# A six-block decoder layer on one NeuronCore: biases padded to 128 rows or moved off TensorE, gathered rows loaded up front, router and context products mixed

## The chip, the cores and the metric

The kernel runs on one core of one Trainium2 chip. The metric is the device time of one execution in microseconds (us), less is better. A core has five engines with instruction streams of their own: TensorE (PE; its weight loads are shown apart as PEld), VectorE (DVE), ScalarE (ACT), GpSimd (POOL) and SyncE (SP, shown as SPq where it issues DMAs). They run side by side and wait for one another by semaphores. All data is fp32, and TensorE runs one fp32 product as two passes, so the profile counts two matmul instructions for one line of code.

## The reference

Input x is (4, 1024, 256), ctx (4, 77, 256); with 128 partitions (P), 4096 tokens are 32 tiles (NT) or 8 chunks (NCH) of 4 tiles (TC). D is 256, in KD = 2 blocks of 128.

```python
x = x + mamba(_layernorm(x))
x = x + gelu_product(_layernorm(x), ctx)     # h = x ctx^T; (gelu(h) * h) ctx
x = x + top1_experts(_layernorm(x))          # 8 experts
x = x + self_attention(_layernorm(x))        # 16 heads, causal
x = x + cross_attention(_layernorm(x), ctx)  # q, k, v, o with biases
x = x + top2_experts(_layernorm(x))          # 8 experts, SwiGLU, 1024 wide

def _L0_ffn_ref(x, router_w, router_b, expert_w, expert_b):
    logits = hs @ router_w + router_b
    probs = softmax(logits);  idx = argmax(probs);  gate = probs[idx]
    return gate * (hs @ expert_w[idx] + expert_b[idx])
```

The second router has a bias of the same kind (`logits = xf @ wg.T + bg`), and cross attention ends in `out @ Wo.T + bo`.

## The kernel before, in words

The residual (`K.resid`, R in the code) stays in SBUF through all stages, [128, 32, 256]. The stages run one after another, each in a block of its own that ends in a barrier of all engines. In a block each engine has its stream written out by hand, and the order in it is fixed.

`_context_and_route` (L913) computes the second residual block and the first router in one loop over chunks. For chunk n TensorE's stream is: `hidden(n)` (xnT by ctxT into pH), the transposes of chunk n+1's normalised rows and of chunk n-1's second normalised rows, `product(n)` (L1260: four tiles of gT by the rows of ctx into pO, which must be added to R before the next one), `logits(n-1)` (L1268: for each of four tiles a bias product with one row, `ones[0:1]` by `router_b`, and two router products into 8 columns), and `places(n-2)` (L1278: prefix counts of the tokens of each expert, with `base`, the first slot of each expert, added by a product with one row). VectorE adds pO to R (L1028), takes statistics of the new rows, finds the largest logit (L1032, L1036), and computes the choice (L1042 to L1056), then the shift (L1018) from which ScalarE normalises (L1182), evaluates Gelu (L1189) and copies the transposed rows (L1174: xnT, hT). VectorE makes gT from it (L1024). The transposes, logits and places share four PSUM banks `pT` in turn (`USES`, `BANKS`); the banks are copied out by ScalarE. Rows go to DRAM sorted by expert by indirect DMAs of GpSimd.

`_expert_units` (L1315) runs the expert product over 39 units of 128 sorted rows, each with one expert's weights. SyncE reads a unit's row and expert number from a table into registers and issues the loads of h (L1347) and w (L1349) into four buffers; ScalarE copies the transposed rows; TensorE does the transposes of the next unit (L1399), then the bias product (L1406) of 8 rows, `mine[:, i]` (1 in the row of the unit's expert) by `b` [8, 256], and the two weight products (L1410). VectorE scales by the gate, GpSimd scatters to `y1_tokens`.

`_project_qkv` (L1435) has chunk loops on all engines: y, the expert output of 4 tiles, is loaded from `y1_tokens` by SyncE (`front`, L1454), added to R by VectorE (`gather`, L1475), normalised and transposed (`LayerNormFront`), projected by q, k and v (L1499, L1502), and v is stored to DRAM by SyncE (`tail`, L1463: four DMAs a chunk). SyncE's order is front(i+1), tail(i). VectorE's order puts the gather and the statistics of chunk i+1 ahead of the evictions of chunk i's first tile.

`_cross_attention` (L2171) is pipelined by tile over 32 tiles. TensorE: transposes and queries, scores, the product with v (L2700), `product` (output bias with one row, L2708, and two products by wo, L2710), the second router (`logits`, L2733 and L2735) and its places. VectorE adds to R (L2323). GpSimd normalises (`normalise`), spreads, and scatters. The sorted rows feed `_expert_slots` (L2811), and `_combine` (L2971) ends the kernel.

## Time and profile before

| | |
|---|---|
| time, median of 3 runs | 3711.72 us (3709.19 to 3711.99) |
| profiled execution | 3711.74 us, span 3709.9 us |
| TensorE busy | 3152.7 us, 85% of the span |
| VectorE busy | 2068.2 us, 56% |
| ScalarE busy | 1450.1 us, 39% |
| GpSimd busy | 1447.2 us, 39% |
| mean granted clock of TensorE | 0.894 of 2.4 GHz |
| DMA | 351.36 MB, mean 95 GB/s |

Stages by the trace: Mamba to about 1037 us, `_context_and_route` to 1213, `_expert_units` to 1366, `_project_qkv` to 1581, self-attention to 2470, `_cross_attention` to 2843, `_expert_slots` to 3665, `_combine` to the end. The granted clock is what the chip's throttle lets TensorE have, as a share of 2.4 GHz; a mean between 0.5 and 1 is a mix of 1.2 and 2.4 GHz. "128*128" in a matmul row is the weight tile, 128 rows contracted by 128 columns; "8*128" is a product that contracts 8 rows. Ends of matmuls are modelled and overlap the next start by some 0.07 us, so durations of groups are best read from start to start.

### The profile page before, as it was taken

The numbers are of one execution on the slowest core, as the hardware profiler recorded it, in microseconds if no ns is written. First come the engines' busy times: TensorE is split into PE (matmuls) and PEld (weight loads), VectorE is DVE, ScalarE is ACT, GpSimd is POOL, SyncE is SP. The second block draws the span as 40 slices with busy tenths as digits, with TensorE's granted clock in tenths as the row PEclk, the third lists the DMA queues.
The fourth block names the chain that finished last, engine by engine and source line by source line (L and its number), as shares of the span: only waits on it lengthen the run. The fifth ranks groups of instructions, "written<-read, shape, count | busy, mean of one in ns | idle before, by whom it ended". The sixth has DMA issues, their size and how long they took to land. (4 is left out here: it accounts for less than half of the span.)

```text
span 3709.9 us, 47740 instructions
## 1 busy us (share of the span) xinstructions
PE 3152.7 (85%) x15459; PEld 2000.7 (54%) x15459; DVE 2068.2 (56%) x3683; ACT 1450.1 (39%) x2767; POOL 1447.2 (39%) x1179
## 2 busy tenths in 40 slices
PE   6899889988778874469999999979995999999995
PEld 2344334433256542235555555546674888888884
DVE  5899999999943122246666666647862212211213
ACT  5667766676423000025545555535541111111110
POOL 4788888877734220023232323235643000000000
PEclk8999999999976557769999999989985999999997
DMA  6224422444001431102222221120003455455454
GB/s 202 80 58 138 139 93 53 130 138 121 18 12 39 140 105 41 37 13 55 53 52 51 52 51 27 30 63 2 19 30 120 162 191 193 158 206 184 163 189 181
DMA packets 278926, 351.36 MB, mean 95 GB/s; under 512 B 84312, under 2 KB 231701, under 8 KB 278757
## 3 DMA queue, kind: packets, MB, share of 16 engines
q1 hardware_dynamic: 264629, 317.82, 28.9%
q0 software_dynamic: 9888, 27.21, 2.0%
q10 hardware_dynamic: 4240, 4.20, 0.3%
q8 instruction: 90, 1.47, 0.2%
q14 instruction: 79, 0.65, 0.1%
HBM read 243.73 MB, written 104.80 MB: 94 GB/s over the span
## 5 line engine op out<-in xcount | busy, mean ns | idle before, releaser
L514 POOL TENSOR_TENSOR mb_drive<-mb_dtx,mb_b_rep 128x1024 f32<-128x1024 f32 x256 | 599.1, 2359 | 179.5 <-DVE mb_pD L437 77.1
L816 PE MATMUL mb_pY<-mb_hc,ident 128*128 128x512 f32 x1024 | 504.1, 617 | 62.7 <-DVE mb_hc L448 62.3
L1693 DVE TENSOR_REDUCE at_nm_of<-at_pS 128x1 f32<-128x512 f32 (+3 forms) x768 | 408.5, 554 | 220.4 <-PE at_pS L1685 121.0
L1761 ACT ACTIVATE at_e<-at_pE 128x512 f32<-128x512 f32 x576 | 325.7, 598 | 349.9 <-PE at_pE L1752 349.4
L2913 DVE TENSOR_TENSOR et_mT<-et_silu,et_pU 128x512 f32<-128x512 f32 (+1 forms) x160 | 100.4, 628 | 560.6 <-ACT et_silu L2887 559.2
L1769 POOL TENSOR_SCALAR_AFFINE_SELECT at_e<-at_e 128x256 f32<-128x256 f32 x256 | 156.4, 629 | 596.3 <-ACT at_e L1761 594.9
L816 PEld LDWEIGHTS mb_pY<-mb_hc,ident 128*128 128x128 f32 x1024 | 190.2, 195 | 337.0 <-issue 179.8
L2887 ACT ACTIVATE et_silu<-et_pG 128x512 f32<-128x512 f32 (+1 forms) x160 | 87.9, 549 | 698.6 <-PE et_pU L2939 642.2
L2872 POOL DMA_INDIRECT t_y_tokens<-et_y,et_to x71 | 68.1, 959 | 750.2 <-DVE et_y L2917 661.4
L1681 PE MATMUL at_pS<-at_kT,at_qT 64*128 64x512 f32 (+3 forms) x768 | 303.5, 445 | 67.1 <-DVE at_nm_of L1693 63.0
L562 ACT ACTIVATE mb_pD<-mb_dt,mb_a_neg 128x512 f32<-128x512 f32 x384 | 259.6, 688 | 154.3 <-DVE mb_hc L448 143.1
L2939 PE MATMUL et_pG<-et_hT,et_wg 128*128 128x256 f32 (+1 forms) x1280 | 289.1, 371 | 34.4 <-issue 26.9
L437 DVE TENSOR_TENSOR_SCAN mb_pD<-mb_pD,mb_carried,mb_drive 128x512 f32<-128x512 f32 x256 | 313.8, 1269 | 7.3 <-ACT mb_pD L562 7.3
L431 DVE TENSOR_TENSOR_SCAN mb_pD<-mb_pD,mb_drive 128x1024 f32<-128x1024 f32 x128 | 292.8, 2287 | 41.2 <-ACT mb_pD L560 38.3
L448 DVE TENSOR_TENSOR mb_hc<-mb_pD,mb_c_rep 128x1024 f32<-128x1024 f32 x256 | 308.1, 1204 | 0.0
L2939 PE MATMUL et_pU<-et_hT,et_wu 128*128 128x256 f32 (+1 forms) x1280 | 276.3, 359 | 0.0
L2939 PEld LDWEIGHTS et_pG<-et_hT,et_wg 128*128 128x128 f32 x1280 | 234.5, 198 | 68.3 <-issue 38.2
L2950 PE MATMUL et_pO<-et_wd,et_mT 128*128 128x256 f32 x1136 | 264.9, 379 | 0.0
L1749 PE MATMUL at_pE<-at_qT,at_kT 64*128 64x512 f32 (+3 forms) x768 | 243.2, 392 | 12.4 <-ACT at_e L1761 12.4
L2939 PEld LDWEIGHTS et_pU<-et_hT,et_wu 128*128 128x128 f32 x1280 | 227.7, 194 | 27.8
L1681 PEld LDWEIGHTS at_pS<-at_kT,at_qT 64*128 64x128 f32 x768 | 135.4, 188 | 198.0 <-DVE at_nm_of L1693 170.7
L2950 PEld LDWEIGHTS et_pO<-et_wd,et_mT 128*128 128x128 f32 x1136 | 211.4, 190 | 26.4
(415 smaller groups left out, 5347.1 us busy)
## 6 DMA issues: line engine op xcount, KB each, us to landing
t_h_sorted<-blank SPq DMA_DIRECT2D x13, 4160.0 KB, 20.3
et_wg<-in_t_wgT SPq DMA_DIRECT2D x40, 1024.0 KB
et_wu<-in_t_wuT SPq DMA_DIRECT2D x40, 1024.0 KB
et_wd<-in_t_wdT SPq DMA_DIRECT2D x40, 1024.0 KB
mb_b_rep<-mb_rows SPq DMA_DIRECT2D x64, 512.0 KB, 5.0
mb_c_rep<-mb_rows SPq DMA_DIRECT2D x64, 512.0 KB, 5.3
eu_w<-in_t_w SPq DMA_DIRECT2D x39, 256.0 KB
t_h_sorted<-blank SPq DMA_DIRECT2D x2, 4290.0 KB, 22.2
```

Source lines behind the costliest of these rows:

```text
L431: nc.vector.tensor_tensor_scan(both(pD), both(pD), both(drive), 0.0, ALU.mult, ALU.add).then_inc(s_scan, 2)
L437: nc.vector.tensor_tensor_scan(pD[r][:, k, :], pD[r][:, k, :], drive[r][:, k, :], carried[:, m, 2 * j + k:2 * j + k + 1], ALU.mult, ALU.ad ...
L448: nc.vector.tensor_tensor(hc[r][:, :, :], pD[r][:, :, :], c_rep[:, 2 * j:2 * j + 2, :], ALU.mult).then_inc(s_hc, 1)
L514: nc.gpsimd.tensor_tensor(drive[G % RINGS][:, :, :], dtx[:, m, :].unsqueeze(1).to_broadcast([P, 2, CH]), b_rep[:, 2 * j:2 * j + 2, :], ALU ...
L562: nc.scalar.activation(pD[r][:, k, :], dt[:, m, :], ACT.Exp, scale=scale).then_inc(s_dec, 1)
L816: last = nc.tensor.matmul(pY[:, :], K.ident[:, :], hc[G % RINGS][:, k, :], start=False, stop=(j == PAIRS - 1 and k == 1))
L1681: last = nc.tensor.matmul(pS[a][:, 0:w1 - w0], qT[b][side(a), h, qb * P:(qb + 1) * P], kT[b][side(a), h, w0:w1], start=True, stop=not diag)
L1693: nc.vector.tensor_reduce(nm_of[:, w0 // 512, a, qb:qb + 1], pS[a][:, 0:w1 - w0], axis=AX.X, op=ALU.max, negate=True).then_inc(s_max, 1)
L1749: nc.tensor.matmul(pE[a][:, at:at + w], kT[b][side(a), h, kb * P:(kb + 1) * P], qT[b][side(a), h, q0:q0 + w], start=(n == 0), stop=False, ...
L1761: nc.scalar.activation(e[g % NE][:, a, :], pE[a][:, :], ACT.Exp).then_inc(s_ex, 1)
L2939: last = nc.tensor.matmul(out[:, x, 0:w * P], weights[:, k, col:col + P], hT[q][:, k, 0:w * P], start=(k == 0), stop=(k == KD - 1))
L2950: last = nc.tensor.matmul(pO[q][:, a, :], mT[j][:, x, a * P:(a + 1) * P], wd[q][:, j * PAIR + x, :], start=(j == 0 and x == 0 and a == 0), ...
```

## The change

In `_context_and_route`, `router_b` is loaded into all 128 partitions and added by VectorE, straight from a PSUM bank `pL` of its own (`pT` keeps three banks); ScalarE's copy of the logits goes. The router products of chunk n-1 are issued between the four tiles of chunk n's context product (`products`). `base` is put into the first running count `sofar[0]`, in one row, and taken off the total at the end. In `_expert_units`, `b`, `number` and `mine` get 128 rows, with zeros behind the eighth, and the bias product contracts 128 rows. In `_project_qkv` y has eight buffers with a semaphore each, and SyncE issues all eight loads ahead of the first store. In `_cross_attention`, `bo` is added to R by GpSimd for a whole chunk (`add_bias`, after `normalise`), `router_b` by VectorE in `best_two`, and both bias products and the base product go; the tables of the places change as in the first router.

```diff
@@ -919,19 +919,19 @@
 
     USES = [(f"LN{k}", 0) for k in range(KD)]
     for n in range(NCH + 2):
-        for name, lag, count in (("LN", -1, KD), ("RT", 1, KD), ("LG", 1, 1), ("PL", 2, 1)):
+        for name, lag, count in (("LN", -1, KD), ("RT", 1, KD), ("PL", 2, 1)):
...
-    BANKS = 4
+    BANKS = 3
...
-        router, router_b = sb("router", [P, KD, NE]), sb("router_b", [1, NE])
+        router, router_b = sb("router", [P, KD, NE]), sb("router_b", [P, NE])
...
-        logit = [sb(f"logit{q}", [P, TC, NE]) for q in range(2)]
+        logit = sb("logit", [P, TC, NE])
...
-        base = sb("base", [1, TC, NE])
...
+        base, token, number, downto = sb("base", [P, NE]), sb("token", [P, NT]), sb("number", [P, UNITS]), sb("downto", [P, NE])
...
-        pO = K.ps(c, "cr_pO", [P, TC, D])
+        pO, pL = K.ps(c, "cr_pO", [P, TC, D]), K.ps(c, "cr_pL", [P, CH])
...
@@ -1028,12 +1027,15 @@
-                eng.wait_ge(s_read, NTH["LG0", ch] + 1)
-                nc.vector.tensor_reduce(top[:, :], logit[ch % 2][:, :, :], axis=AX.X, op=ALU.max).then_inc(s_top, 1)
+                eng.wait_ge(s_L, ch + 1)
+                nc.vector.tensor_tensor(logit[:, :, :], pL[:, 0:TC * NE].rearrange("p (t e) -> p t e", e=NE),
+                                        router_b[:, :].unsqueeze(1).to_broadcast([P, TC, NE]), ALU.add).then_inc(s_logit, 1)
+                eng.wait_ge(s_logit, ch + 1)
+                nc.vector.tensor_reduce(top[:, :], logit[:, :, :], axis=AX.X, op=ALU.max).then_inc(s_top, 1)
...
+                ch.do(nc.vector.tensor_tensor(count[:, :], count[:, :], base[:, :], ALU.subtract))
...
-            nc.vector.memset(sofar[0][:, :], 0.0)
+            nc.vector.memset(sofar[0][:, :], 0.0).then_inc(s_zero, 1)
+            eng.wait_ge(s_zero, 1)
             for x in range(NE):
-                nc.vector.memset(base[:, :, x], float(x * REGION))
+                nc.vector.memset(sofar[0][0:1, x:x + 1], float(x * REGION))
+                nc.vector.memset(base[:, x:x + 1], float(x * REGION))
...
@@ -1221,9 +1220,10 @@
                 if n + 1 < NCH:
                     queries(n + 1)
                 if 1 <= n <= NCH:
+                    if n > 1:
+                        eng.wait_ge(s_L, n - 1)
                     for k in range(KD):
                         turned(hT, "RT", n - 1, k)
-                    logits(n - 1)
                     exponential(n - 1)
...
-            def product(ch):
-                eng.wait_ge(s_g, ch + 1)
-                if ch > 0:
-                    eng.wait_ge(s_res, ch)
+            def products(n):
+                if n < NCH:
+                    eng.wait_ge(s_g, n + 1)
+                    if n > 0:
+                        eng.wait_ge(s_res, n)
+                if n > 0:
+                    eng.wait_ge(s_read, NTH["RT1", n - 1] + 1)
+                    if n > 1:
+                        eng.wait_ge(s_logit, n - 1)
                 for t in range(TC):
-                    last = nc.tensor.matmul(pO[:, t, :], gT[ch % 2][:, t * P:(t + 1) * P], ctx_rows[:, ch // CPB, :], start=True, stop=True)
-                last.then_inc(s_o, 1)
-
-            def logits(ch):
-                out = turn("LG0", ch)
-                eng.wait_ge(s_read, NTH["RT1", ch] + 1)
-                for t in range(TC):
-                    of_t = out[:, t * NE:(t + 1) * NE]
-                    nc.tensor.matmul(of_t, ones[0:1, :], router_b[:, :], start=True, stop=False)
-                    for k in range(KD):
-                        last = nc.tensor.matmul(of_t, hT[:, k, t * P:(t + 1) * P], router[:, k, :], start=False, stop=(k == KD - 1))
-                last.then_inc(s_A, 1)
+                    if n < NCH:
+                        last = nc.tensor.matmul(pO[:, t, :], gT[n % 2][:, t * P:(t + 1) * P], ctx_rows[:, n // CPB, :], start=True, stop=True)
+                        if t == TC - 1:
+                            last.then_inc(s_o, 1)
+                    if n > 0:
+                        for k in range(KD):
+                            last = nc.tensor.matmul(pL[:, t * NE:(t + 1) * NE], hT[:, k, t * P:(t + 1) * P], router[:, k, :],
+                                                    start=(k == 0), stop=(k == KD - 1))
+                        if t == TC - 1:
+                            last.then_inc(s_L, 1)
...
-                nc.tensor.matmul(part(0, TC), ones[0:1, :], base[:, :, :].rearrange("p t e -> p (t e)"), start=True, stop=False)
-                nc.tensor.matmul(part(0, TC), before[:, :], pick[:, :, :].rearrange("p t e -> p (t e)"), start=False, stop=False)
+                nc.tensor.matmul(part(0, TC), before[:, :], pick[:, :, :].rearrange("p t e -> p (t e)"), start=True, stop=False)
...
-                if n < NCH:
-                    product(n)
-                if 1 <= n <= NCH:
-                    logits(n - 1)
+                if n <= NCH:
+                    products(n)
@@ -1322,8 +1322,8 @@
         sem = lambda n: K.sem(c, f"eu_{n}")
         w = [sb(f"w{q}", [P, KD, D]) for q in range(BUFS)]
         h = [sb(f"h{q}", [P, ROW]) for q in range(BUFS)]
-        b = sb("b", [NE, D])
-        number, mine = sb("number", [NE, 1]), sb("mine", [NE, UNITS])
+        b = sb("b", [P, D])
+        number, mine = sb("number", [P, 1]), sb("mine", [P, UNITS])
...
-            eng.dma_start(b[:, :], io["t1_b"]).then_inc(s_in, 16)
+            eng.wait_ge(s_set, 3)
+            eng.dma_start(b[0:NE, :], io["t1_b"]).then_inc(s_in, 16)
...
-            eng.wait_ge(s_set, 2)
-            nc.vector.tensor_scalar(mine[:, :], table["expert_f"][0:NE, :], number[:, 0:1], None, ALU.is_equal).then_inc(s_mine, 1)
+            nc.vector.memset(b[:, :], 0.0).then_inc(s_set, 1)
+            eng.wait_ge(s_set, 3)
+            nc.vector.tensor_scalar(mine[:, :], table["expert_f"][:, :], number[:, 0:1], None, ALU.is_equal).then_inc(s_mine, 1)
...
-                nc.tensor.matmul(pY[q][:, :], mine[:, i:i + 1].to_broadcast([NE, P]), b[:, :], start=True, stop=False)
+                nc.tensor.matmul(pY[q][:, :], mine[:, i:i + 1].to_broadcast([P, P]), b[:, :], start=True, stop=False)
@@ -1441,22 +1443,22 @@
-        y = [sb(f"y{p}", [P, TC, D]) for p in range(2)]
+        y = [sb(f"y{i}", [P, TC, D]) for i in range(NCH)]
...
-            def front(i, p):
-                if i >= 2:
-                    eng.wait_ge(s_add, i - 1)
+            def gathered(i):
                 src = K.y1_tokens[0:TOK, :].rearrange("(p t) d -> p t d", p=P)[:, i * TC:(i + 1) * TC, :]
-                eng.dma_start(y[p][:, :, :], src).then_inc(s_y[p], 16)
-            front(0, 0)
+                eng.dma_start(y[i][:, :, :], src).then_inc(s_y[i], 16)
+
+            gathered(0)
...
+            for i in range(1, NCH):
+                gathered(i)
             for i in range(NCH):
-                if i + 1 < NCH:
-                    front(i + 1, (i + 1) % 2)
                 tail(i, i % 2)
...
-            eng.wait_ge(s_y[p], 16 * (i // 2 + 1))
-            nc.vector.tensor_tensor(rows(K.resid, i), rows(K.resid, i), y[p][:, :, :], ALU.add).then_inc(s_add, 1)
+            eng.wait_ge(s_y[i], 16)
+            nc.vector.tensor_tensor(rows(K.resid, i), rows(K.resid, i), y[i][:, :, :], ALU.add).then_inc(s_add, 1)
@@ -2196,8 +2198,8 @@
-        bv, bo = sb("bv", [P, D]), sb("bo", [1, D])
-        router, router_b = sb("router", [P, KD, NE]), sb("router_b", [1, NE])
+        bv, bo = sb("bv", [P, D]), sb("bo", [P, D])
+        router, router_b = sb("router", [P, KD, NE]), sb("router_b", [P, NE])
...
-        base = sb("base", [1, TC, NE])
+        base = sb("base", [P, NE])
@@ -2320,6 +2323,8 @@
             def add(n):
                 eng.wait_ge(s_O, n + 1)
+                if n % TC == 0:
+                    eng.wait_ge(s_bo, n // TC + 1)
                 nc.vector.tensor_tensor(R[:, n, :], R[:, n, :], pO[:, 0:D], ALU.add).then_inc(s_res, 1)
...
+                nc.vector.tensor_tensor(logit[ch % 2][:, :, :], logit[ch % 2][:, :, :], router_b[:, :].unsqueeze(1).to_broadcast([P, TC, NE]),
+                                        ALU.add).then_inc(s_logit, 1)
+                eng.wait_ge(s_logit, ch + 1)
...
+            def add_bias(ch):
+                of_chunk = R[:, ch * TC:(ch + 1) * TC, :]
+                eng.wait_ge(s_xn[0], (ch + 1) * TC)
+                nc.gpsimd.tensor_tensor(of_chunk, of_chunk, bo[:, :].unsqueeze(1).to_broadcast([P, TC, D]), ALU.add).then_inc(s_bo, 1)
...
+            eng.wait_ge(s_in, ALL_IN)
+            for ch in range(2):
+                add_bias(ch)
...
                 if ch is not None:
                     deviation(0, ch)
                     normalise(ch)
+                    add_bias(ch)
@@ -2705,9 +2725,8 @@
-                nc.tensor.matmul(pO[:, 0:D], ones[0:1, :], bo[:, :], start=True, stop=False)
                 for k in range(KD):
-                    last = nc.tensor.matmul(pO[:, 0:D], mixedT[n % 2][:, k, :], wo[:, k, :], start=False, stop=(k == KD - 1))
+                    last = nc.tensor.matmul(pO[:, 0:D], mixedT[n % 2][:, k, :], wo[:, k, :], start=(k == 0), stop=(k == KD - 1))
...
-                    nc.tensor.matmul(of_t, ones[0:1, :], router_b[:, :], start=True, stop=False)
                     for k in range(KD):
-                        last = nc.tensor.matmul(of_t, hT[:, k, t * P:(t + 1) * P], router[:, k, :], start=False, stop=(k == KD - 1))
+                        last = nc.tensor.matmul(of_t, hT[:, k, t * P:(t + 1) * P], router[:, k, :], start=(k == 0), stop=(k == KD - 1))
...
-                nc.tensor.matmul(part(0, TC), ones[0:1, :], base[:, :, :].rearrange("p t e -> p (t e)"), start=True, stop=False)
-                nc.tensor.matmul(part(0, TC), before[:, :], pairs[:, :, :].rearrange("p t e -> p (t e)"), start=False, stop=False)
+                nc.tensor.matmul(part(0, TC), before[:, :], pairs[:, :, :].rearrange("p t e -> p (t e)"), start=True, stop=False)
```

## Rows read from the trace of the kernel before

**Rows 1.** Table of busy times by stretch; columns as in its first line.
```profile
core 0: us, PE busy (x) PEld busy (x) DVE busy (x) ACT busy (x) POOL busy (x), PEclk, DMA share, GB/s
1029.00:1213.00 184.00, 139.19 (x540) 107.17 (x538) 73.94 (x326) 61.24 (x113) 68.42 (x69) 0.64 0.08 27
1366.00:1581.00 215.00, 106.42 (x320) 61.32 (x320) 59.34 (x177) 20.62 (x48) 8.16 (x9) 0.74 0.14 43
1103.20:1118.00 14.80, 13.36 (x57) 10.41 (x56) 6.70 (x28) 6.58 (x12) 8.66 (x8) 0.65 0.11 37
1220.00:1340.00 120.00, 120.00 (x269) 71.78 (x269) 23.45 (x99) 12.31 (x33) 31.66 (x33) 0.50 0.50 149
960.00:1000.00 40.00, 22.71 (x47) 7.86 (x47) 40.00 (x36) 14.36 (x23) 29.38 (x14) 1.00 0.00 1
2588.00:2744.00 156.00, 155.05 (x1234) 109.16 (x1233) 121.10 (x307) 76.27 (x148) 84.33 (x75) 0.89 0.06 22
```

**Rows 2.** Waits from 1366 to 1581: in total, times, longest.
```profile
DVE resid L1477 <- DMA qk_y<-t_y_tokens: 95.8, 7, 14.2
```

**Rows 3.** Timeline of TensorE in `_expert_units`: start, us, instruction.
```profile
1226.05 1.22 PE L1406 MATMUL eu_pY<-eu_b,eu_mine 8*128 8x256 f32 x2
1227.20 2.08 PE L1410 MATMUL eu_pY<-eu_w,eu_hT 128*128 128x256 f32 x4
1229.06 0.64 PE L1399 MATMUL eu_pT<-ident,eu_h 128*128 128x128 f32 x2
```

**Rows 4.** The page's costliest groups: busy, mean ns, idle before.
```profile
L514 POOL TENSOR_TENSOR mb_drive<-mb_dtx,mb_b_rep 128x1024 f32<-128x1024 f32 x256 | 599.1, 2359 | 179.5 <-DVE mb_pD L437 77.1
L816 PE MATMUL mb_pY<-mb_hc,ident 128*128 128x512 f32 x1024 | 504.1, 617 | 62.7 <-DVE mb_hc L448 62.3
```

**Rows 5.** Timeline of SyncE at the start of `_expert_units`.
```profile
1215.82 0.35 SPq L1347 DMA_DIRECT2D eu_h<-t_h_sorted  x1
...
1218.08 0.34 SPq L1347 DMA_DIRECT2D eu_h<-t_h_sorted  x1
```

**Rows 6.** Timeline of `_project_qkv`, near chunk 1 and at the end.
```profile
1388.89 1.04 PE L177 MATMUL qk_pT<-ident,qk_xn 128*128 128x128 f32 x8
...
1392.34 1.88 PE L1499 MATMUL qk_pQK<-qk_w,qk_xnT 128*128 128x512 f32 x4
...
1392.94 5.41 SPq L1467 DMA_DIRECT2D sa_v_dram<-qk_v_rows  x4
...
1407.54 1.22 DVE L1477 TENSOR_TENSOR resid<-resid,qk_y 128x1024 f32<-128x1024 f32 x1 [14.25 <-DMA qk_y<-t_y_tokens]
...
1565.75 0.37 ACT L1515 COPY qk_v_rows<-qk_pV 128x256 f32<-128x256 f32 x1 [2.21 <-PE qk_pV L1502]
...
1580.92 1.29 SPq L2025 DMA_DIRECT2D at_wo<-in_sa_woT  x3
```

**Rows 7.** Stretch of 1 us behind the stores: ScalarE busy, clock, DMA share, GB/s.
```profile
1405.00:1406.00 1.00, 0.00 (x0) 0.50 0.14 52
```

**Rows 8.** Timeline of one round of `_context_and_route`.
```profile
1101.25 1.99 PE L1265 MATMUL cr_pO<-cr_ctx_rows,cr_gT 77*128 77x256 f32 x8 [1.47 <-DVE cr_gT L1024]
...
1104.55 1.02 PE L1275 MATMUL cr_pT<-cr_router,cr_hT 128*128 128x8 f32 x4
...
1113.28 2.08 ACT L1182 ACTIVATE cr_rows<-resid,cr_shift,cr_rstd 128x256 f32<-128x256 f32 x4 [1.74 <-issue]
...
1118.03 1.99 PE L1265 MATMUL cr_pO<-cr_ctx_rows,cr_gT 77*128 77x256 f32 x8 [1.47 <-DVE cr_gT L1024]
1118.10 1.08 ACT L1174 COPY cr_hT<-cr_pT 128x512 f32<-128x512 f32 x2
```

**Rows 9.** Timeline of TensorE in `_cross_attention`, around the second router.
```profile
2614.01 0.69 PE L2708 MATMUL xa_pO<-xa_bo,xa_ones 1*128 1x256 f32 x2
...
2619.03 0.38 PE L2733 MATMUL xa_pT<-xa_router_b,xa_ones 1*128 1x8 f32 x2
2619.34 0.61 PE L2735 MATMUL xa_pT<-xa_router,xa_hT 128*128 128x8 f32 x4
...
2623.88 1.21 PE L2708 MATMUL xa_pO<-xa_bo,xa_ones 1*128 1x256 f32 x2
```

More of the change, by code:

```diff
@@ L1035, in below @@
                     eng.wait_ge(s_e, ch)
[L1036 removed]
+                nc.vector.tensor_tensor(behind[:, :, :], logit[:, :, :], top[:, :].unsqueeze(2).to_broadcast([P, TC, NE]),
                                         ALU.subtract).then_inc(s_behind, 1)
@@ L1447, in _project_qkv @@
         s_in, s_mm, s_q, s_v = (sem(n) for n in ("in", "mm", "q", "v"))
-        s_out, s_y = ([sem(f"{n}{p}") for p in range(2)] for n in ("out", "ys"))
+        s_out = [sem(f"out{p}") for p in range(2)]
+        s_y = [sem(f"ys{i}") for i in range(NCH)]
         s_add = sem("add")
@@ L2397, in make_table @@
                 eng.wait_ge(s_read, NTH["CN0", 0] + 1)
+                ch.do(nc.vector.tensor_tensor(count[:, :], count[:, :], base[:, :], ALU.subtract))
                 ch.do(nc.vector.tensor_scalar(steps[:, :], number[:, 0:32], float(P), None, ALU.mult))
@@ L2450, in _ @@
             nc.vector.memset(before[:, :], 1.0)
-            nc.vector.memset(sofar[0][:, :], 0.0)
+            nc.vector.memset(sofar[0][:, :], 0.0).then_inc(s_zero, 1)
+            eng.wait_ge(s_zero, 1)
             nc.vector.memset(twos[:, :], 0.0)
             for x in range(NE):
-                nc.vector.memset(base[:, :, x], float(x * REGION))
+                nc.vector.memset(base[:, x:x + 1], float(x * REGION))
+                nc.vector.memset(sofar[0][0:1, x:x + 1], float(x * REGION))
             nc.vector.memset(v[:, :, :, :, :], 0.0).then_inc(s_set, 1)
```

16 lines of the change are left out of this document (5 added, 11 removed).

## The prediction

> **What bounds the kernel now.** I read the table of busy times by stretch first [rows 1], over the four stages that the change touches. Call them A (context product and first router, 1029 to 1213 us), B (39 expert units, to 1366), C (the q, k, v projection, to 1581) and E (cross attention and second router, 2470 to 2843). The Mamba stage before A, the self-attention between C and E, and the slot experts and combination after E keep their instructions; I cost them at nothing, since every stage ends in a barrier.
>
> B: TensorE is busy without a gap (120.00 of 120.00 us) while its granted clock is 0.50, that is 1.2 of 2.4 GHz. C: TensorE works half the time; VectorE waits 95.8 us for the gathered rows [rows 2], and TensorE stands behind it. A: a ring of waits through all engines, TensorE at a mean clock of 0.64. E: TensorE is the bound (155.05 of 156.00 us), clock 0.89; VectorE is next at 121.10 [rows 1].
>
> **Part B, biases padded to 128 rows.** 33 units in 120 us are 3.6 us each [rows 1]: the two 8-row bias products 1.15, the four weight products 1.86 (0.465 each), two transposes the rest, 0.57 [rows 3]. Padding moves no column: six full products and the transposes would take 3.36, 0.22 a unit less, 8 us in all. The larger term is the clock. Does it rise? Late in Mamba TensorE was busy only 22.71 of 40 us and its clock was 1.00 [rows 1]; its products there have 128 rows [rows 4]. B is busier and stays at 0.50, with a third of its time in 8-row products. The difference that I see is the rows, so I take it that padding lets the clock rise. A unit then costs TensorE about 1.7 and it isn't the bound any more. What is late next is SyncE: while nothing held it back, it needed 2.26 us from one load of rows to the next [rows 5], with the weights and the register reads of a unit between them. So B goes at 2.27 a unit: 35 units that now wait save 1.31 each, 46, and the backlog of four loaded units at the end drains in half the time, 7 more: 53. Against it: the DMA share rises from 0.50 [rows 1] to 0.50 x 3.6 / 2.27 = 0.79, so landings get later; I take off 5 for that: **B -48**, bounds -53 and 0. The bias tile's new memset and the DMA behind it are over before the first weights land; hidden.
>
> The Trainium skill, page "TensorE: Matmul & The Clock Gate" (Part 1, The HAM clock gate), says that the gate follows how busy TensorE has been of late, and names no rows. By that rule B would be at full clock already; the trace disagrees, 120 busy us at 0.50. If it were the rule after all, padding would change nothing, which is the rival "clock stays" below.
>
> **Part C, all gathered rows loaded up front.** Before, the load of chunk i+1 is issued behind the four stores of chunk i-1's v rows on SyncE (1392.94 to 1398.35), the rows are there at 1407.54, and VectorE, which must gather chunk i+1 before it evicts chunk i, idles 14.25 us [rows 6]. Seven such waits make the 95.8 [rows 2]. After it, the loads have eight buffers. The next limit is TensorE: a tile takes 2.58 us at full clock (ScalarE's copy, 0.37, and its wait, 2.21), eight transposes 1.04 less the overlap of the ends, about 0.9 [rows 6], a chunk 11.2. VectorE has 59.34 us for 8 chunks [rows 1], 7.4 each, and keeps up. Chunk 1's first tile starts at 1392.34 as now, the clock having risen by then; 28 tiles and six groups of transposes later it is 1392.3 + 72.2 + 5.4 = 1470. The v stores move at 52 GB/s [rows 7]: 512 KB a chunk take 10.1 us, just under 11.2, so they keep pace, and the stage ends 15.2 us behind the last v copy as now (1565.75 to 1580.92) [rows 6]: 1485, **C -96**. Bounds: -100, and -60 if stores or landing order bind. The 4 MB of loads in front need 28 us at B's 149 GB/s [rows 1] and are through about when the first store starts; their seven more issues, ahead of the stores on SyncE, come in the 25 us in which SyncE has nothing else.
>
> At 1405 the stores run with a DMA share of 0.14 [rows 7], about 2 of 16 engines. The skill's page "DMA: Bandwidth & Descriptors" (Rules for kernel authors) says that a transfer whose outermost dimension is small runs on that many engines; this one's is 2, and the trace agrees. By that rule the stores, not the loads, are C's next bound, whatever is loaded early.
>
> **Part A.** Removed per chunk: eight 1-row router bias steps and two base steps on TensorE, 0.26 us each at the low clock. But the ring is re-ordered. Now VectorE's residual add starts after the eight steps of the context product, 1.99 us at full clock, and the router steps come behind it, 0.255 each at the low clock (4 in 1.02) [rows 8]. Afterwards the product also waits for ScalarE's two hT copies (to 1119.18, 1.15 us later than now), and its eight steps are mixed with 16 router steps, 12 of them ahead of the last one. So the add starts after 8 x 0.24 + 12 x 0.14 = 3.6 at full clock (0.14 from 4 in 0.61 less the overlap of ends [rows 9]), 8 x 0.465 + 12 x 0.255 = 6.8 at the low one. From the add to the shift VectorE has 6.7 busy between 1103.20 and 1118.00 [rows 1], less 0.7 for gT, plus 0.6 for the new bias add: 6.6. From the shift (ScalarE at 1113.28) through table load and Gelu to the hT copies: 5.9 [rows 8]. Sum 16.1 at full clock, 19.3 at the low one, against 16.8 now (1101.25 to 1118.03). The other new waits, ScalarE's hT copies for the last router products and TensorE's for the last bias add, are met a round earlier. With hidden and context products apart by that much I expect the clock low more often than not: 18 on the mean, +1.2 for seven chunks = +8, less 3 in the last two rounds, where bias and base steps fall away with nothing beside them: **A +5**, bounds -7 and +17.
>
> **Part E.** Removed on TensorE: per tile the output bias, 0.62 at full clock (0.69 less the overlap), 1.1 at the low one; per chunk four router bias pairs of 0.31 (2619.03 to 2619.34) [rows 9] and a base pair alike. Per chunk 3 x 0.62 + 1.1 + 5 x 0.31 = 4.5 of 39 (156 / 4); eight chunks 36. The clock now drops once a chunk, behind the router steps (the same bias pair takes 0.69 before them and 1.21 after [rows 9]); a mean of 0.89 means 22% of 39 us at 1.2 GHz, of which full clock would give back 4.3, less 0.9 counted above. I take half of it, since 16 router steps stay: 1.7 for six chunks, 10. Cost: GpSimd's bias add, 128x1024, 2.36 us by a like shape [rows 4], once a chunk. GpSimd has 84.33 of 156 us busy [rows 1], 21 of 39, so its slack hides that, but VectorE may wait for its small operations while it runs: 1 us a chunk, 8. VectorE is at 30.3 of 39 and gets a small router add, so it allows no less than about 31. The residual add now also waits for the bias add of its chunk, with VectorE's statistics queued behind it; GpSimd issues that ten tiles ahead: nothing. -36 - 10 + 8: **E -38**, bounds -15 and -58. The wider broadcast loads of the biases: within 0.5.
>
> **Sum.** The profiled execution took 3711.74 us (span 3709.9), the median of three is 3711.72, so I sum against 3711.7: +5 - 48 - 96 - 38 = -177, **3535**.
>
> **Rivals.**
> Clock stays low in B. For it: B's load is steady and heavy, and no other stretch shows what 8 rows do. B -15, rest as above: 3568. Chance 0.15.
> Clock recovers everywhere: A at 16.1 a chunk (-7 for my +5), E with all of its 3.4 a chunk (-10 more): 3513. Chance 0.18.
> C bound by its DMAs: from 1392.94 to 1407.54 one chunk's stores and one load took 14.6 [rows 6]; at that pace C is 23 longer: 3558. Chance 0.10.
> E doesn't follow: VectorE and GpSimd, both near 30 of 39, hold each other, E -15: 3558. Chance 0.05.
> Slower: the mixed order keeps TensorE at 1.2 GHz, as in A (0.64). Place: E above all. A chunk there is 39 x 0.89 = 34.7 us of full-clock work, 31.1 without its biases; at a mean clock of 0.66 it takes 47, +64. With it A +17, B 0 and C at 22.5 a chunk, -9: +72, 3784. It decides once E's mean clock is under 0.8 (31.1 / 0.8 = 39). Against it: C's bursts reach full clock today. Chance 0.02.
> That the change doesn't do what it says: the loads in C wait for nothing any more in the code, so only the clock can fail, and that is priced.
>
> **How the numbers follow.** My forecast has 0.50 and, by its own bounds, 3510 to 3560. The range for 8 in 10 takes in the clock rivals and the DMA one, and most of C's and B's bounds: **3498 to 3590**. Faster by over 0.2% (7.4 us, about what a measurement of this kernel can tell from no change): 0.97; within it 0.01; slower 0.02.
>
> **What the profile after would show.** B: clock near 1.00, 2.3 us a unit, SyncE waiting for nothing; wrong if TensorE is still gapless at 0.50. C: no wait of resid for t_y_tokens after chunk 1, TensorE gapless at 11.2 a chunk, the end 15 behind its last. A: the residual add 3.6 to 6.8 us behind the product's start, chunks 16 to 19 apart. E: 33 to 35 us a chunk, with or without a clock drop behind the router steps. If C lasts over 120 us, or B over 110, the sum is off by as much.

## The result, and the profile after

The changed kernel takes 3604.39 us (median of 4, 3599.18 to 3608.14) against 3711.85 for the kernel before beside it, a ratio of 0.971 (95% interval 0.969 to 0.973). The forecast was 3535, with a range from 3498 to 3590. So the gain is 107 us instead of 177, and the time lies above the range.

I cut both profiled executions at the first operation of each stage (for A the first row statistics, for B the first load of h, for C that of y, for self-attention its first memset, and so on); all times in this table are us.

| stage | before | after | difference | forecast |
|---|---|---|---|---|
| Mamba | 1039.0 | 1043.4 | +4.4 | 0 |
| A, context product and first router | 174.0 | 179.1 | +5.1 | +5 |
| B, expert units | 152.8 | 109.9 | -42.9 | -48 |
| C, q, k, v projection | 215.2 | 118.5 | -96.7 | -96 |
| self-attention (its code is not changed) | 891.8 | 960.6 | **+68.8** | 0 |
| E, cross attention and second router | 380.4 | 328.7 | -51.7 | -38 |
| slot experts | 822.3 | 830.4 | +8.1 | 0 |
| combination | 34.4 | 35.8 | +1.4 | 0 |
| span | 3709.9 | 3606.4 | -103.5 | -177 |

The four changed stages gave -186 together, near the forecast of -177 (the two stages of 4.4 and 8.1 and the combination take 14 of it back). What went wrong is a stage that the diff doesn't touch. Over all 16 profiles of this study, whose Mamba and slot-expert code is the same, Mamba takes 1034.4 to 1045.6 and the slot experts 814.5 to 833.0, so their two differences are within their own spread; that of self-attention isn't.

The table of busy times by stretch, of the kernel after (columns as in [rows 1]), stages A, B, C, self-attention and E:

```profile
1043.40:1222.50 179.10, 123.50 (x434) 92.66 (x434) 72.40 (x316) 58.38 (x103) 68.99 (x69) 0.57 0.08 28
1222.50:1332.40 109.90, 71.73 (x312) 52.78 (x312) 27.80 (x117) 14.51 (x39) 37.41 (x39) 0.90 0.65 188
1332.40:1450.90 118.50, 93.14 (x320) 56.88 (x320) 58.80 (x176) 20.60 (x48) 8.14 (x9) 0.87 0.22 78
1451.00:2411.00 960.00, 802.00 (x5921) 470.92 (x5921) 543.36 (x1093) 427.55 (x800) 270.60 (x387) 0.92 0.21 43
2411.50:2740.20 328.70, 268.64 (x2346) 192.95 (x2346) 256.76 (x715) 153.15 (x299) 214.90 (x191) 0.87 0.10 32
```

The same of the kernel before, self-attention and E, which don't stand in [rows 1] as whole stages:

```profile
1581.00:2472.00 891.00, 782.18 (x5921) 457.17 (x5921) 542.22 (x1086) 425.82 (x800) 270.81 (x387) 0.95 0.23 45
2472.80:2853.20 380.40, 328.49 (x2490) 234.22 (x2490) 255.17 (x706) 154.33 (x299) 196.16 (x183) 0.82 0.08 28
```

Self-attention runs the same 5921 matmuls in 69 us more, at a clock of 0.92 instead of 0.95. The waits of its TensorE after, 1451 to 2411 (total, times, longest), and below them those before:

```profile
PE at_pS L1683 <- DVE at_nm_of L1695: 62.3, 123, 1.2
PE at_pE L1751 <- issue: 49.4, 6, 9.2
```
```profile
PE at_pS L1681 <- DVE at_nm_of L1693: 63.0, 125, 1.2
...
PE at_pE L1749 <- ACT at_e L1761: 12.4, 34, 0.7
```

The second line is new: six times TensorE waits up to 9.2 us for nothing that the profile shows ("issue"). Before, no such line is there, and the same instruction waits 12.4 in 34 short waits for ScalarE. One of the six in the timeline (start, us, instruction, idle before):

```profile
1895.02 1.27 PE L1805 MATMUL at_pO<-at_e,at_v 128*32 128x512 f32 x12
1903.71 0.79 PE L1751 MATMUL at_pE<-at_qT,at_kT 64*128 64x512 f32 x1 [7.42 <-issue]
```

All six stand at this place, 113 to 118 us apart, and this is the place where TensorE's hardware loop (four tiles a pass, seven passes, so six returns) goes back to its first instruction. The stretches around it (TensorE busy, clock, DMA share, GB/s), and of one whole pass:

```profile
1890.00:1896.00 6.00, 5.77 (x50) 1.00 0.55 157
1896.00:1898.00 2.00, 0.29 (x6) 1.00 1.10 229
1900.00:1902.00 2.00, 0.00 (x0) 0.50 1.08 275
1904.00:1908.00 4.00, 4.00 (x19) 0.50 1.08 265
1908.00:1912.00 4.00, 4.00 (x22) 0.50 1.00 154
1912.00:1920.00 8.00, 7.04 (x50) 0.96 0.01 2
...
1903.70:2021.60 117.90, 99.77 (x740) 0.92 0.22 46
```

The clock falls while TensorE stands and is still 0.50 until about 1912, so a return costs more than its wait of 7.4 to 9.2: 68.8 / 6 = 11.5 on the mean. And the page's list of DMA queues shows what is fetched, before and after:

```profile
q8 instruction: 90, 1.47, 0.2%
```
```profile
q8 instruction: 142, 2.33, 0.3%
```

52 packets more, of 16 KB each (1.47 MB / 90), all of them instructions. The changed kernel without the waits (after_fill161 below) has 89, so the six returns cost 53. From 1800 to 2300 us, between the first and the last return, there are none in the kernel before, and after there are

```profile
q8 instruction: 38, 0.62, 0.6%
```

They come two at the return and seven more while the pass runs.

The other parts, after. A: the eight product steps mixed with router steps, at the low clock (the two steps of a tile take 0.98 from start to start); the residual add starts 6.35 behind the product, in seven of eight rounds:

```profile
1089.58 1.19 PE L1271 MATMUL cr_pO<-cr_ctx_rows,cr_gT 77*128 77x256 f32 x2 [0.88 <-ACT cr_hT L1179]
1090.56 0.86 PE L1276 MATMUL cr_pL<-cr_router,cr_hT 128*128 128x8 f32 x4
...
1095.93 1.22 DVE L1027 TENSOR_TENSOR resid<-resid,cr_pO 128x1024 f32<-128x1024 f32 x1 [6.21 <-PE cr_pO L1271]
```

B: the busy times of its middle, and the one wait of TensorE in it:

```profile
1230.00:1320.00 90.00, 65.24 (x289) 48.01 (x289) 25.58 (x108) 13.39 (x36) 33.81 (x36) 0.94 0.72 208
```
```profile
PE eu_pT L1401 <- DMA eu_h<-t_h_sorted: 24.7, 27, 3.2
```

36 units in 90 us are 2.50 each, with the clock at 0.94 where it was 0.50 [rows 1]. C: SyncE issues the seven loads within 4.25 us, the stores run from 1359, and TensorE's last product ends at 1436.03, 14.8 ahead of the next stage:

```profile
1334.27 4.25 SPq L1459 DMA_DIRECT2D qk_y<-t_y_tokens  x7
1358.97 83.33 SPq L1469 DMA_DIRECT2D sa_v_dram<-qk_v_rows  x32
1450.84 1.29 SPq L2027 DMA_DIRECT2D at_wo<-in_sa_woT  x3
```
```profile
1435.00 1.03 PE L1504 MATMUL qk_pV<-qk_w,qk_xnT 128*128 128x256 f32 x4
```

### The profile page after: what moved, and what is told of

Its sections match the earlier page's. It is cut to its first block and busy times, and to the rows that moved or that the text cites. A ratio compares the mean times of both kernels' runs of the same rounds, so it can differ in the third digit from the quotient of the medians.

```text
span 3606.4 us, 47336 instructions
## 1 busy us (share of the span) xinstructions
PE 3029.5 (84%) x15235; PEld 1932.1 (54%) x15235; DVE 2070.6 (57%) x3718; ACT 1448.6 (40%) x2759; POOL 1466.2 (41%) x1187
## 5 line engine op out<-in xcount | busy, mean ns | idle before, releaser
L1751 PE MATMUL at_pE<-at_qT,at_kT 64*128 64x512 f32 (+3 forms) x768 | 250.6, 400 | 61.8 <-issue 49.4
```

Source lines behind the costliest of these rows:

```text
L1751: nc.tensor.matmul(pE[a][:, at:at + w], kT[b][side(a), h, kb * P:(kb + 1) * P], qT[b][side(a), h, q0:q0 + w], start=(n == 0), stop=False, ...
```

## The experiments

### Where the 69 us come from

TensorE's loop has 1738 instructions in the built program (a pass has 740 matmuls, the (x740) above, each with its weight load, and 258 register operations and waits). Part A takes 161 TensorE instructions away ahead of it, in stages that come earlier. By my count the loop starts 7680 instructions into TensorE's program before, and 7519 after.

The Trainium skill, page "Runtime: NRT & Kernel Launch" (Instruction fetch mechanics), gives TensorE an instruction memory of 128 KiB, 2048 instructions, that is refilled in blocks of 16 KiB, 256 instructions. The same section says that a taken branch whose target lies outside the current window of two pages forces a fetch of the target page. The size of the packets agrees. A window of two pages doesn't: 1738 instructions are nearly seven blocks, and in the kernel before six returns over them wait for nothing and bring no packet. My theory, which is not the page's: a loop that lies over seven blocks stays resident and one that lies over eight doesn't, and 7680 is 30 x 256. What a return that waits brings is nine packets: 27 more than before with three such returns, 36 with four, 54 with six (before_fill40, before_fill25, before_fill95 below). Nine blocks are more than the whole loop, so it is fetched anew, and not only its first block. The resident size itself no run measured.

Fillers serve as a probe: waits of TensorE for a semaphore that has long been set, two to an instruction.

```diff
             nc.tensor.transpose(pF[0][:, 0:P], order_row[:, :], K.ident[:, :]).then_inc(s_oT, 1)
+            for _ in range(2 * 161):
+                eng.wait_ge(s_ord, 1)
```

> The changed kernel with 161 instructions more on TensorE, waits for a semaphore that has long been set, put behind the first transpose of the self-attention stage, where TensorE idles 12.8 us for a DMA. Theory (code position): the stage is 69 us longer in the changed kernel (960.6 against 891.8) because part A has 161 TensorE instructions less ahead of its loop, and the loop of 1738 instructions, which began on a multiple of 256 instructions, now begins 161 earlier and covers eight stretches of 256 instead of seven; each of six returns to its top then waits 7.4 to 9.2 us. With the position restored the six waits are gone, the stage takes 891 to 893, all else stays: 3604 - 69 = 3535. Rival (the state in which the stage begins, its buffers' places, or the clock): the stage stays at 961 and the kernel at 3604, or 3610 if the fillers cost.

Measured 3525.8 (ratio to before 0.951, 0.948 to 0.954), self-attention 901.5, no wait at the return. The six waits are gone, and the instruction packets are 89. Of the 9 us over 892 the fillers explain 4.9: TensorE's idle time there is 17.4 instead of 12.8, and its first scores come 4.9 later in the stage. The rest isn't located; other runs without waits have self-attention at 891.8 to 896.9. That the place of the loop makes the waits holds, and with it the forecast for the rest.

> The kernel before with 95 such fillers at the same place and nothing of the change. 95 more stand in the same place against a multiple of 256 as 161 fewer. Theory (code position): self-attention 961 us, with six waits of 7 to 9 us at the loop's return, the kernel at 3712 + 69 = 3781. Rival (something else of the change): 3712 to 3717.

(95 in place of 161, in the kernel before.) Measured 3784.65 (1.021, 1.018 to 1.023), self-attention 970.2 (expected 961), and six waits at the same place in a kernel that has nothing of the change:

```profile
PE at_pE L1749 <- issue: 45.2, 6, 7.8
```

> The changed kernel with the context and first router stage (part A) of the kernel before; B, C and E as changed. Theory (code position): TensorE has its 161 instructions back, so self-attention is back at 892 and this stage at 174 instead of 179: 3604 - 69 - 5 = 3530. Rival (B, C or the new layout slow the self-attention): it stays at 961, and the kernel at 3599.

(`_context_and_route` as a whole from the kernel before.) Measured 3516.33 (0.949, 0.947 to 0.951), self-attention 892.2, A 172.7. Nothing in B, C or E slows self-attention; the place in the program does.

Where is the edge? Three runs of the kernel before with 40, 25 and again 40 fillers, and one of the changed kernel with 150 at the end of C:

```diff
             emit("tensor", eng)
+            for _ in range(2 * 150):
+                eng.wait_ge(s_mm, 1)
```

> The kernel before with 40 fillers. The loop has 1738 instructions, and seven stretches of 256 are 1792, so it can start up to 54 behind a multiple. Theory (code position, the loop of before starting on a multiple, as my count of the program has it): 40 still fit, self-attention stays at 892, the kernel at 3712. If the count is off by more than 14 or if any shift costs: 961, 3781.

> The changed kernel with 150 fillers at the end of C: by my count the loop starts 11 instructions ahead of a multiple of 256 and covers eight stretches again. Theory (code position, with before's loop exactly on the multiple): six waits of 7 to 9 us, self-attention 961, total 3604. If the count is off by more than 11, the loop fits: 892, 3535.

> The kernel before with 25 fillers. So far a start 11 ahead of that of before had no wait at the loop's return, 40 behind had three of six, 95 behind all six. Theory (the loop's last instruction must stay some way ahead of a boundary that lies at about 40 behind): 25 has none, self-attention 892 to 895, total 3706. Rival (any start behind that of before costs something): one to three waits of 7 to 8 us, 900 to 917.

> The same kernel as the one with 40 fillers, run again. Theory (near the edge it is a race between how far the fetch has run ahead and the return, so its outcome differs from execution to execution): another number of waits than three, or other returns than the first, third and fifth. Rival (the position alone sets it): three again, at the same returns, self-attention 917.

| start against before's | kernel | returns that wait | self-attention | time |
|---|---|---|---|---|
| -161 | after | 6 of 6 | 960.6 | 3604.39 |
| -11 | after_fill150 | 0 | 892.1 | 3515.37 |
| 0 | before, old_router_stage | 0 | 891.8, 892.2 | 3711.85, 3516.33 |
| +25 | before_fill25 | 4 (1st, 2nd, 5th, 6th) | 943.8 | 3762.0 |
| +40 | before_fill40, before_fill40_again | 3 (2nd, 4th, 6th) | 917.2, 929.3 | 3740.61, 3750.46 |
| +95 | before_fill95 | 6 of 6 | 970.2 | 3784.65 |

The rows for -11, +25 and +40 are single executions. My expectation for +40 (none, since seven blocks would leave 54), for -11 (six) and for +25 (none) all failed. So my count of blocks doesn't give the edges: one lies between 0 and 25 behind, the other between 11 and 161 ahead, where nothing was run. That +25 has more waits than +40 also speaks against a simple threshold. Which returns wait isn't chance at +40: the second run has its three waits at the same returns (the second, fourth and sixth; the expectation above calls them the first, third and fifth). But its stage is 12 us longer, at a clock of 0.928 instead of 0.947 and with waits of 6.5 to 6.7 instead of 6.9 to 8.0, so the place doesn't fix the cost. What pattern of refills gives four and three of six stays open.

What sets the length? The DMA share is 1.10 through the wait above, since SyncE issues a write of 4 MB of blanks, once a pass, about 4 us ahead of TensorE's return.

```diff
                 for x in range(FULL, FULL + TURN):
+                    if x == FULL + 2:
+                        eng.dma_start(blanks[:, bass.ds(j * each, each), :], many.to_broadcast([P, each, ROW])).then_inc(s_blanks, 16)
                     sync(eng, j * TURN + x, x)
-                eng.dma_start(blanks[:, bass.ds(j * each, each), :], many.to_broadcast([P, each, ROW])).then_inc(s_blanks, 16)
```

> The changed kernel, loop position unchanged (all six returns wait), but the 4 MB write of blanks in self-attention is issued in the middle of SyncE's loop body instead of at its end. In the changed kernel it is issued some 4 us before TensorE's return, and the DMA share is 1.1 through the whole wait. Theory A (the fetch of instructions queues behind the blanks, which sets the 7.4 to 9.2 us): the six waits shrink to 1 to 4 us, the clock stays up through most of them, self-attention takes 900 to 925. Theory B (the wait is the fetch's own time): still 7 to 9 us, 955 to 965.

Measured, in one execution: six waits still, with 142 instruction packets as after, but short ones, 2.3 to 2.7:

```profile
PE at_pE L1751 <- issue: 14.8, 6, 2.7
```

Self-attention takes 919.6 and the kernel 3564.11. The packets show why. After, TensorE stops at 1661.50, no instruction packet starts until 1665, and two do behind that; with the blanks moved, it stops at 1660.10, and two have started in the 3 us before. The instruction queue from 1665 to 1670 after, and from 1657 to 1660 with the blanks moved:

```profile
q8 instruction: 2, 0.03, 5.0%
```
```profile
q8 instruction: 2, 0.03, 4.7%
```

So of the 68.8 us some 41 are the fetch standing behind the blanks and the clock that falls meanwhile. The other 28 are waits of 14.8 and, by an estimate, the clock: 919.6 x (1 - 0.938) = 57 us lost to it, against 891.8 x (1 - 0.954) = 41 before. That moving the blanks changes nothing else in the stage was not tested; no run has them moved without the waits.

### B: what lets the clock rise

```diff
-        b = sb("b", [P, D])
-        number, mine = sb("number", [P, 1]), sb("mine", [P, UNITS])
+        b = sb("b", [32, D])
+        number, mine = sb("number", [32, 1]), sb("mine", [32, UNITS])
```

(with the selector's and the table's slices to match; 64 in the second run). The first run also cuts C's stores, the second also changes E; each stage is read for itself. As wholes they measured 3557.34 (0.959, 0.956 to 0.963) and 3558.81 (0.960, 0.957 to 0.964).

> The run with the old router stage, with two stages edited that are read apart. B: the bias tile, its row numbers and the selector have 32 rows instead of 128. Theory (the clock goes by how many rows TensorE's products fill): 32 rows in a third of the work is nearer to 8 than to 128, the clock stays mostly at 1.2 GHz and B takes 130 to 145 us. Rival (anything above the 8 rows of before is enough, or it is the work's pace and not rows): 107 as with 128 rows. C: each v store is cut in two, whose outermost dimension is 64 rows instead of 2 (64 issues instead of 32). Theory (the old form runs on 2 of 16 DMA engines and its last chunk ends 15 us behind TensorE): the tail shrinks to 3 to 5 us, C 107 instead of 118 to 119. Rival (the tail is the writes' latency or SyncE's issue): 118, or more if 8 issues a chunk of 0.6 us hold SyncE. Total by the theories: 3516 + 30 - 11 = 3535.

> The run with the old router stage, with two stages edited that are read apart. B: the bias tile with 64 rows. Theory (rows): clock mostly up, B 107 to 115. Rival: as with 8 rows, 145. E: the output bias is a TensorE product again, with 128 rows (each 1/128 by the bias broadcast) instead of 1, and GpSimd's bias add is gone; the router bias stays on VectorE. Theory 1 (E went from 380 to 325 mostly by work taken off TensorE): two passes of 256 columns, 0.46 us at full clock, 0.93 at the low one, come back for each of 32 tiles, 15 to 20 us, less up to 8 for GpSimd: 332 to 345. Theory 2 (it was mostly the clock, which 128 rows keep as well): 325 to 330.

In a third the bias product is left out:

> The changed kernel with unmixed router products, and with the expert bias product of B left out altogether (the expert biases are then missing from the result); 156 fillers more keep the loop's position. Theory (the 8-row product was what held the clock down): no low-row product is left, the clock is up at 0.85 to 1.00, B 105 to 108, bound by SyncE. Rival (the clock of B needs the 128-row product's activity, that is, more filled columns): the clock stays near 0.50, a unit costs TensorE 2.4 and B takes 108 to 115, so the clock and TensorE's busy time tell the two apart, not the stage's time.

Stage B of the three, 32 rows, 64 rows and none (columns as in [rows 1]):

```profile
1219.40:1372.10 152.70, 140.11 (x312) 82.85 (x312) 27.76 (x117) 14.51 (x39) 37.39 (x39) 0.50 0.45 135
```
```profile
1207.30:1333.80 126.50, 103.86 (x312) 59.19 (x312) 27.76 (x117) 14.53 (x39) 37.54 (x39) 0.74 0.55 163
```
```profile
1188.10:1294.40 106.30, 62.81 (x234) 42.10 (x234) 27.74 (x117) 14.53 (x39) 37.41 (x39) 0.82 0.66 194
```

With 32 rows TensorE is busy without a gap at 1.2 GHz, as with 8:

```profile
1225.00:1365.00 140.00, 139.12 (x310) 82.27 (x308) 27.44 (x115) 14.14 (x38) 36.43 (x38) 0.50 0.47 142
```

32 rows are as slow as 8 (152.7 and 152.8), 64 are between, and 128 give 106.4 to 109.9 in the eight runs that have them, at a clock of 0.90 to 0.95. Without any bias product the clock is 0.82 and the stage takes 106.3 (that run, one execution, takes 3501.65, with 317 fillers that outlast C). That is a little under the 0.85 to 1.00 of the theory and far from the 0.50 of the rival. So it is the rows of the product that count, and not that there is one: the same 312 matmuls of the same columns stay at 1.2 GHz with 8 and with 32 rows. Why 32 give nothing and 64 a part stays open. The Trainium skill's page "TensorE: Matmul & The Clock Gate" (Part 1, The HAM clock gate) has the gate follow how busy TensorE has been; with 8, 32 and 64 rows TensorE is busiest and its clock is lowest, so the runs disagree with it as it stands there. My figure for 32 rows (130 to 145) was too good, that for 64 (107 to 115) as well; the order was right.

### C: the stores

```diff
-                    eng.dma_start(of_pair[t % 2], v_rows[p][:, t, :]).then_inc(s_out[p], 16)
+                    for h in range(2):
+                        at = i * CH + (t // 2) * 2 * P + h * P + (t % 2) * (P // 2)
+                        eng.dma_start(v_dram[at:at + P // 2, :], v_rows[p][h * (P // 2):(h + 1) * (P // 2), t, :]).then_inc(s_out[p], 16)
```

In rows32_stores64, C takes 111.7 instead of 119.4 (old_router_stage; 118.5 after), at a DMA share of 0.28 instead of 0.22. TensorE's last product ends 104 into the stage in both, and the tail behind it fell from 15.5 to 7.4. The store's form did hold the end of the stage, as the theory said, though 7.7 came back and not 11 and the tail isn't down to 3 to 5:

```profile
1372.10:1483.80 111.70, 93.76 (x320) 57.24 (x320) 58.79 (x176) 20.60 (x48) 8.15 (x9) 0.90 0.28 83
```

### E: work taken away, or clock

rows64_bias128 has E at 336.8 against 324.9 of old_router_stage, which it is compared with: a 128-row bias product on TensorE costs 12 us more than GpSimd's add, at the same mean clock of 0.87. That lies inside the 332 to 345 of theory 1, but it doesn't show its "mostly". With the output bias's work back on TensorE the stage is still 43.6 under the 380.4 of before. By the prediction's price the router bias and base products are 5 x 0.31 x 8 = 12 of that, so about 31, an estimate, is the clock (0.82 to 0.87) and whatever else changed. Of the 55.5 that E gained in old_router_stage, the removed work of both kinds is about 24. No run keeps the 1-row products and takes only work away.

### A: mixed or not

```diff
                     if n > 0:
                         eng.wait_ge(s_res, n)
+                    for t in range(TC):
+                        last = nc.tensor.matmul(pO[:, t, :], gT[n % 2][:, t * P:(t + 1) * P], ctx_rows[:, n // CPB, :], start=True, stop=True)
+                    last.then_inc(s_o, 1)
                 if n > 0:
                     eng.wait_ge(s_read, NTH["RT1", n - 1] + 1)
...
                 for t in range(TC):
-                    if n < NCH:
-                        last = nc.tensor.matmul(pO[:, t, :], gT[n % 2][:, t * P:(t + 1) * P], ctx_rows[:, n // CPB, :], start=True, stop=True)
```

> The changed kernel, with the router products of a chunk behind its four context products, as in the kernel before, instead of between them; VectorE's bias add and the own bank stay. The loop's position is made good by 161 fillers at the end of TensorE's stream in C, where it idles 15 us. Theory (A's loss is that the residual add waits for the mixed router products at a low clock): the add starts 2 to 3.7 us after the product's start instead of 6.4, but the product steps lose nothing else: A 165 to 171 instead of 179, self-attention 892, total 3516 - 5 = 3511 to 3516. Rival (the loss is the later start behind the hT copies, or a clock that falls without the mix): A 176 to 182.

Measured 3494.49 (0.942, 0.939 to 0.945); A takes 150.9, and 148.5, 148.1 and 148.0 in three later runs, against 177.9 to 179.1 mixed (four profiles) and 164.7 to 174.0 for the old stage (eight). The mean clock over A is 0.66 to 0.67 unmixed, 0.57 to 0.60 mixed and 0.62 to 0.65 for the old stage, so the clock is lowest with the mix. The timeline of two rounds, at the low and at the full clock:

```profile
1083.23 3.62 PE L1266 MATMUL cr_pO<-cr_ctx_rows,cr_gT 77*128 77x256 f32 x8
1086.65 3.42 PE L1274 MATMUL cr_pL<-cr_router,cr_hT 128*128 128x8 f32 x16
1086.89 1.22 DVE L1027 TENSOR_TENSOR resid<-resid,cr_pO 128x1024 f32<-128x1024 f32 x1 [2.44 <-PE cr_pO L1266]
...
1099.16 1.89 PE L1266 MATMUL cr_pO<-cr_ctx_rows,cr_gT 77*128 77x256 f32 x8
...
1101.09 1.22 DVE L1027 TENSOR_TENSOR resid<-resid,cr_pO 128x1024 f32<-128x1024 f32 x1 [0.30 <-PE cr_pO L1266]
```

The add starts 3.7 or 1.9 us behind the product's start instead of 6.35, and this round takes 15.9 instead of 18.6 (1089.58 to 1108.17). I had expected 165 to 171: the direction was right, the size too small. The edit undoes two things at once, the mix and the product's wait for hT, so this run doesn't part the theory from the rival's "later start behind the hT copies". The trace of the kernel after bounds the second: the wait is 0.77 to 1.03 us a round, 6.4 of the 27 to 31 in all. The rival's other half, a clock that falls without the mix, is refuted, since it rose.

### All of it together

> The changed kernel with what the runs so far found: router products behind the context products, the v stores cut so that their outermost dimension is 64, and the loop of self-attention brought back by 161 fillers at the end of C. Theory (the stages end in barriers and their gains add up): A 151, B 107 to 110, C 111.5, self-attention 892 to 896, E 325; the run with unmixed products less 7.5 for C: 3487. Rival (A's 151 was one lucky pattern of the clock): A 165 to 171, 3502 to 3507.

Measured 3485.04 (0.941, 0.938 to 0.944): A 148.1, B 108.9, self-attention 893.4, E 322.6, but C 117.2, since its 161 fillers outlast the stores' tail once that is short.

> As the run with unmixed products and stores cut in two, but with 150 fillers instead of 161 (the run with 150 had no wait at the loop's return), 42 of them at the end of C and 108 in the self-attention stage where TensorE idles 12.8 us. Theory (a filler costs TensorE about 0.09 us: C ended at 117.2 with 161 of them and at 111.7 without, self-attention began 9.3 later with 161): both idle times now hide their share, C 112, self-attention 892 to 895, total 3485 - 5 = 3480. Rival (C's 117.2 has another cause): no change, 3485.

Measured 3483.64 (0.938, 0.936 to 0.941): C 111.5, self-attention 893.0. In the whole the two can't be told apart; in C the 5.7 us are there. It has the lowest time of this study, 230 us under the kernel before where the change alone gave 107.

## Why the prediction was wrong, point by point

**The stages not touched, "I cost them at nothing".** This is the step that failed. That every stage ends in a barrier keeps the order of its work from changing, but not where its instructions lie. +68.8, shown by after_fill161, before_fill95 and old_router_stage. What stood in its place is the loop's place among the instructions that TensorE fetches: nine packets and 7.4 to 9.2 us of wait at each of six returns. With it made good the changed kernel takes 3515.37 (after_fill150, one execution) to 3525.8 (where the fillers cost some time themselves), inside the range and within 20 of the 3535. The 3535 and the 68.8 together come within 1 us of the measured 3604.39, which is luck: E gave 14 more than forecast, B 5 less, and Mamba and the slot experts took 12.5 within their spread.

**A, +5.** Measured +5.1, and step by step as forecast: the add 6.35 behind the product's start at the low clock (6.8 forecast), rounds of 16.2 to 19.0 (16 to 19), the clock down from 0.62 to 0.57 over the stage. That it is 5.1 to the decimal is luck: the old stage takes 164.7 to 174.0, and before is at its upper end. The step was a sum of a gain and a loss that I didn't price apart. router_unmixed did: without the mix and the wait for hT the stage is 22 under the old one (150.9 against 172.7), so the two cost 27 to 31.

**B, -48.** Measured -42.9. The clock rose for the reason given, and the rival "clock stays" fell. The new bound was named only in part: SyncE's own pace is 2.27 [rows 5], but a unit takes 2.50. TensorE's 24.7 of 90 us are waits for rows, at a DMA share of 0.72; at 2.27 a unit they would be 90 x (1 - 1.81 / 2.27) = 18, with 65.24 / 36 = 1.81 busy. Mostly SyncE itself is slower: it issues the loads of rows 2.53 apart on the mean, the fifth to the last, and waits 4.2 us for a free buffer. I had taken off 5; against the 53 it was 10. Part of that is this execution, which has the longest B of the eight with 128 rows (106.4 to 109.9). What slows SyncE otherwise no run shows.

**C, -96.** Measured -96.7, in its forecast shape: all loads issued by 1338.5, one wait for y at the start, the end 14.8 behind the last v copy (15.2). The rival "bound by its DMAs" fell.

**E, -38.** Measured -51.7, inside the bounds to -58. Two terms were off. The clock: in the steady middle it went to 0.96 where I had taken half of the way from 0.89, and a chunk took 31.3 to 32.4 us instead of 33 to 35:

```profile
2526.00:2682.00 156.00, 148.87 (x1399) 107.67 (x1397) 140.48 (x367) 87.76 (x174) 109.80 (x95) 0.96 0.09 30
```

Over the whole stage, by an estimate, TensorE lost 380.4 x (1 - 0.82) = 68 us to it before and 328.7 x (1 - 0.87) = 43 after, so 25 came back where I had 10 and some 7 inside the removed steps. And the 8 us for VectorE waiting on small operations of GpSimd aren't there: no wait for GpSimd is among its seven largest. Its wait for TensorE ahead of the residual add fell from 52.3 to 16.0, as these two lines show (E before, E after). The mechanism was right, the sizes of two terms not.

```profile
DVE resid L2323 <- PE xa_pO L2710: 52.3, 18, 8.4
```
```profile
DVE resid L2328 <- PE xa_pO L2729: 16.0, 10, 4.5
```

**The range.** It had no case for a stage that isn't touched. Its upper end, 3590, was 14 short.

## What to carry to other kernels

A diff moves every instruction that stands behind it on the same engine: where a kernel has a long hardware loop (1738 instructions here), count the instructions ahead of it before and after, look in the profile for "issue" waits at the loop's return and at the packets of the instruction queue, and keep large transfers away from the return. A product with few rows can hold the clock of a busy TensorE down, and filling up its missing rows with zeros made the stage 43 us shorter. Where a change mixes two groups of steps to help the clock, ask who waits for the last step of the first group, and price gain and loss apart.

## What the runs showed of the hardware that I had not expected

Six returns of one TensorE loop cost 69 us, and 95 instructions that only wait for what has long happened make a kernel 2.1% slower (1.8 to 2.3). A return that waits fetches nine blocks of 16 KB, one that doesn't none. The fetch of instructions stands behind other DMA traffic: 7.4 to 9.2 us a return beside a 4 MB write, 2.3 to 2.7 without. A filler costs TensorE about 0.11 us (156 more at the end of C, 134.7 against 117.2). The granted clock of a TensorE without gaps was 0.50 with 8 or 32 rows in a third of its work; with 64 it was 0.74 over the stage, with few gaps; with 128 rows it was 0.90 to 0.95, TensorE then having gaps.
